# A two-layer vision block on one core: the last pass keeps the first one's token order

## The reference

```
x = x + L0_conv(_ln_c(x))     # 8x8 windows shifted by (4, 4), 12 heads of 8, cosine scores,
                              # a position bias made from a small MLP, a mask across the shift
t = t + L0_ffn(_ln_t(t))      # weights binarized in 5 groups; outputs scaled by the absolute
                              # maximum over 3 images (images 0 to 14 in 5 groups; image 15 gets 0)
x = x + L1_conv(_ln_c(x))     # q = x @ w_q; a 3x3 grouped convolution of q, layer norm, gelu;
                              # offset = tanh(t @ w_offp) * (8, 8); k and v from a bilinear sample
                              # of x at position + offset; 12 heads over all 256 tokens
t = t + L1_ffn(_ln_t(t))      # 4 experts of 384, the best 2 by softmax gate
```

## Time and profile before

| | us |
|---|---|
| three runs | 1008.96, 1015.61, 1023.27 |
| median | 1015.61 |
| profiled execution | 1014.97 |
| its span, first to last instruction | 1013.1 |
| TensorE busy, matmuls | 802.2 (79%) |
| VectorE, ScalarE, GpSimd busy | 490.8, 444.0, 354.3 |
| mean granted TensorE clock | 0.925 of full speed |

### The profile page before, as it was taken

One profiled execution on the slowest core, in us unless ns is written; L12 is line 12 of the kernel. 1 busy time (PEld: TensorE's weight loads), 2 busy tenths in 40 slices (PEclk: granted clock), 3 DMA queues, 4 the chain that ended last, 5 costly groups with the idle time before them and its releaser, 6 DMA issues.

```text
span 1013.1 us, 27125 instructions
## 1 busy us (share of the span) xinstructions
PE 802.2 (79%) x11232; PEld 622.7 (61%) x11232; DVE 490.8 (48%) x1080; ACT 444.0 (44%) x690; POOL 354.3 (35%) x866
## 2 busy tenths in 40 slices
PE   3466776276828875897799898499999999999998
PEld 2345555164616753675777666377777787776766
DVE  3244454263428616674536733455664465465411
ACT  0233352152305431752585483145435444553573
POOL 3335445353424504631512221224423322331233
PEclk9999888597959996998899998799999899999999
DMA  7000000004003033510130400442144044404000
GB/s 218 23 2 4 3 3 7 20 2 103 6 20 85 21 80 90 126 44 19 40 69 6 102 4 25 114 103 68 41 105 106 13 95 106 99 22 91 6 6 12
DMA packets 23450, 53.45 MB, mean 53 GB/s; under 512 B 9552, under 2 KB 18080, under 8 KB 21280
## 3 DMA queue, kind: packets, MB, share of 16 engines
q1 hardware_dynamic: 22752, 51.47, 21.3%
q10 hardware_dynamic: 576, 0.25, 0.1%
HBM read 45.40 MB, written 6.30 MB: 51 GB/s over the span
## 4 chain that ended last, share of the span: by engine, by line
PE 38%; DMA 7%; issue 4%; DVE 4%; SPq 3%; POOL 3%; ACT 2%; POOLq 0%; ACTq 0%; DVEq 0%
PE ps L1214 35%; DMA hx<-hat_scratch 5%; SPq L473 3%; PE ps L1221 1%; DVE nmx L936 1%; DMA hat_scratch<-hat 1%; ACT prob L1169 1%; DVE hat L917 0%; DVE hat L916 0%; DMA x_all<-x_scratch 0%; ACT L1169 0%; PE ps L1476 0%; PE ps L1270 0%; PE ps L1506 0%; ACT L1196 0%
## 5 line engine op out<-in xcount | busy, mean ns | idle before, releaser
L936 DVE TENSOR_REDUCE nmx<-ps 128x4 f32<-128x1024 f32 x96 | 114.4, 1220 | 50.2 <-PE ps L1214 49.8
L1196 ACT ACTIVATE hidden<-ps 128x512 f32<-128x512 f32 x96 | 57.2, 597 | 142.2 <-PE ps L1214 141.9
L1214 PE MATMUL ps<-turned_x,we 128*128 128x256 f32 x384 | 104.6, 397 | 0.0
L1214 PE MATMUL ps<-we,hidden 128*128 128x96 f32 x768 | 103.4, 287 | 0.7 <-ACT hidden L1196 0.7
L1214 PEld LDWEIGHTS ps<-we,hidden 128*128 128x128 f32 x768 | 96.9, 200 | 11.0 <-issue 7.1
L1169 ACT ACTIVATE prob<-ps 128x1024 f32<-128x1024 f32 x96 | 93.5, 1025 | 16.3 <-PE ps L1214 15.4
L545 POOL TENSOR_SCALAR veps_c<-mv_c 128x2 f32<-128x2 f32 x32 | 9.3, 290 | 235.5 <-DVE mv_c L711 235.2
L1214 PEld LDWEIGHTS ps<-turned_x,we 128*128 128x128 f32 x384 | 67.4, 194 | 17.0 <-issue 7.6
L1214 PE MATMUL ps<-wconv,xpp 128*128 128x96 f32 x576 | 71.6, 286 | 4.2 <-POOL xpp L631 3.7
L1214 PE MATMUL ps<-u_turned 32*64 32x64 f32 x3072 | 52.9, 238 | 27.1 <-DVE nmx L936 17.7
L1214 PEld LDWEIGHTS ps<-wconv,xpp 128*128 128x128 f32 x576 | 69.8, 202 | 7.1 <-POOL xpp L631 4.1
(11 more groups left out here) (230 smaller groups left out, 1616.4 us busy)
## 6 DMA issues: line engine op xcount, KB each, us to landing
hx<-hat_scratch SPq DMA_DIRECT2D x16, 1536.0 KB, 12.7
hy<-hat_scratch SPq DMA_DIRECT2D x16, 768.0 KB, 5.9
hat_scratch<-hat SPq DMA_DIRECT2D x32, 96.0 KB, 1.9
x_scratch<-x_all SPq DMA_DIRECT2D x128, 6.0 KB
x_all<-in_x SPq DMA_DIRECT2D x4, 384.0 KB, 4.3
x_all<-x_scratch SPq DMA_DIRECT2D x16, 96.0 KB, 1.9
out<-u_hid SPq DMA_DIRECT2D x16, 96.0 KB, 1.7
x_scratch<-x_all SPq DMA_DIRECT2D x64, 12.0 KB
```

What stands on the lines that cost most here:

```text
L936: v.tensor_reduce(dst, src, AX.X, ALU.max, negate=True).then_inc(sem("c_mx"), 1)
L1196: a.activation(hidden[:, 2 * k:2 * k + 2, :].rearrange("p m n -> p (m n)"), ps[:, k % 2, :], ACT.Gelu).then_inc(sem("c_h"), 1)
L1214: return m.matmul(o, l, r, start=start, stop=stop)
```

## The change

1. **The host's layout is read and written in window order to the end.** Within a window the 64 tokens are now numbered row by row (`j // 8`, `j % 8`; before, four columns at a time), and the result is put back into raster order by the host. `leave`, `back`, `x2_scratch` and the semaphores for them are gone; `c_st` waits for `b_x2` (or `a_x1` for image 15) instead.
2. **The convolution's raster copy is made on chip.** `c_xt` transposes the two tiles twice, the second time with a reordered output; `c_xnt` copies the first result to a new tile `cxt`, which `c_q` reads; a new ScalarE piece `c_xp` makes `xpp` from the second with four copies, turning rows and columns by the shift.
3. **The coordinates come back in another form.** `hx` now has one tile's size and `hy` two: six transfers of 64 partitions each, in place of two of 128.
4. **Set-up functions are tied to pieces of image 0** (`run`), so that `a_xt(0)`, `a_xnt(0)` and others no longer stand behind them; `table_2` is half as many flip matmuls, twice as wide. The convolution's weights have a semaphore of their own (`inw`) and are folded at image 4, not 2.
5. **All five tables are new.** Two lines of `PLAN_PE`:

The diff, cut to its core:

```diff
@@ tiles
-        hx = sb("hx", [P, TILES * DG * TOK])
-        hy = sb("hy", [P, DG * TOK])
+        hx = sb("hx", [P, DG * TOK])
+        hy = sb("hy", [P, TILES, DG * TOK])
+        cxt = sb("cxt", [P, TOK])
@@ run
-            for n, (_, name, i) in enumerate(turns(plan)):
-                for f in set_up.get(n, ()):
-                    f()
+            for _, name, i in turns(plan):
+                if i == 0:
+                    for f in set_up.get(name, ()):
+                        f()
                 pieces[name](i)
@@ SyncE
-            def leave(i):
-                w("b_x2" if fed(i) else "a_x1", i)
-                image = x2_dram[TOK * i:TOK * i + TOK, :].rearrange("(r c) k -> r c k", c=SIDE)
...
-                            sp.dma_start(image[a0:a0 + rows, c0:c0 + 4, :], x_all[p0:p0 + 4 * rows, i, t, :]).then_inc(landed("x2_out", i), 16)
-
-            def back(i):
-                sp.wait_ge(*at("x2_out", i))
-                w("x_back", i - 1)
-                sp.dma_start(x_all[:, i], x2_dram[TOK * i:TOK * i + TOK, :].rearrange("(p t) k -> p t k", t=TILES)).then_inc(sem("x_back"), 16)
@@ hin
-                yrow = bass.AP(d.tensor, d[0].offset, [[DG * TOK, SIDE], [0, 8], [1, DG * TOK]])
-                xrow = bass.AP(d.tensor, d[1].offset, [[0, SIDE], [2 * DG * TOK, 8], [1, 2 * DG * TOK]])
-                sp.dma_start(hy[:], yrow).then_inc(landed("hat_in", i), 16)
-                sp.dma_start(hx[:], xrow).then_inc(landed("hat_in", i), 16)
+                line = DG * TOK
+                for win in range(2):
+                    part = slice(WIN * win, WIN * win + WIN)
+                    cols = bass.AP(d.tensor, d[1].offset + 8 * win * line, [[0, 8], [line, 8], [1, line]])
+                    sp.dma_start(hx[part, :], cols).then_inc(landed("hat_in", i), 16)
+                    for t in range(TILES):
+                        rows = bass.AP(d.tensor, d[0].offset + 8 * t * line, [[line, 8], [0, 8], [1, line]])
+                        sp.dma_start(hy[part, t, :], rows).then_inc(landed("hat_in", i), 16)
@@ GpSimd
             def c_sh(i):
-                pool.wait_ge(*at("c_xnt", i))
+                pool.wait_ge(*at("c_xp", i))
...
-                     c_ln3=c_ln3, c_rank=c_rank, c_acc=c_acc), PLAN_POOL, {1: [late]})
+                     c_ln3=c_ln3, c_rank=c_rank, c_acc=c_acc), PLAN_POOL, {"a_ln2": [late]})
@@ VectorE
             def c_st(i):
-                dve.wait_ge(*at("x_back", i))
+                w("b_x2" if fed(i) else "a_x1", i)
...
-            run(pieces, PLAN_DVE, {1: [weights_1, weights_2, weights_3, bias_8]})
+            run(pieces, PLAN_DVE, {"a_ss": [weights_1], "a_qn": [weights_2], "a_mx": [weights_3, bias_8]})
@@ ScalarE
             def c_xnt(i):
                 act.wait_ge(*at("c_xt", i))
-                w("c_q", i - 2)
+                w("c_q", i - 1)
+                a.copy(cxt[:], ps[:, 2, 0:TOK]).then_inc(sem("c_xnt"), 1)
+
+            def c_xp(i):
+                act.wait_ge(*at("c_xt", i))
                 w("c_conv", i - 2)
-                a.copy(xpp[:, i % 2, 1:3, 8:8 + P], ps[:, 2, 0:TOK].rearrange("p (a n) -> p a n", a=2)).then_inc(sem("c_xnt"), 1)
+                half, low = SIDE // 2, SHIFT // 2
+                turned_rows = ps[:, 2, TOK:2 * TOK].rearrange("p (r n a) -> p a r n", a=2, n=half)
+                planes = xpp[:, i % 2, 1:3, 8:8 + P].rearrange("p a (r n) -> p a r n", n=half)
+                for r0, r1, rt in ((0, SIDE - SHIFT, SHIFT), (SIDE - SHIFT, SIDE, 0)):
+                    for n0, n1, nt_ in ((0, half - low, low), (half - low, half, 0)):
+                        a.copy(planes[:, :, rt:rt + r1 - r0, nt_:nt_ + n1 - n0], turned_rows[:, :, r0:r1, n0:n1]).then_inc(sem("c_xp"), 1)
...
-            run(pieces, PLAN_ACT, {0: [table_1, table_2, bias_exp, signs]})
+            run(pieces, PLAN_ACT, {"a_xnt": [table_1], "a_qt": [table_2], "a_nmt": [bias_exp], "a_ot": [signs]})
@@ TensorE
-                    for ch in range(2):
-                        src = ebraw[:, 6 * b:6 * b + 6, :].rearrange("p h (r c) -> p h r c", c=15)[:, :, :, 4 * ch:4 * ch + 4]
-                        for h in range(6):
-                            ins = mm(ps[:, 6 + b, WIN * h + 32 * ch:WIN * h + 32 * ch + 32], flip[:], src[:, h])
+                    src = ebraw[:, 6 * b:6 * b + 6, :].rearrange("p h (r c) -> p h r c", c=15)[:, :, :, 0:8]
+                    for h in range(6):
+                        ins = mm(ps[:, 6 + b, cols(h, WIN)], flip[:], src[:, h])
...
-                banks.take([2], "c_xnt", i)
-                turn(2, pads["c_xn"][:, i % 2]).then_inc(sem("c_xt"), 1)
+                banks.take([2], "c_xp", i)
+                src = pads["c_xn"][:, i % 2]
+                turn(2, src)
+                for t in range(TILES):
+                    o = ps[:, 2, TOK + P * t:TOK + P * t + P].rearrange("p (r w n) -> p w r n", r=8, w=2)
+                    ins = m.transpose(o, src[:, t, :], ident[:])
+                ins.then_inc(sem("c_xt"), 1)
...
-                    ins = mm(flat(0, 1024)[:, cols(g, TOK)], wqs[:, g, :], xpp[:, i % 2, 1:3, 8:8 + P])
+                    ins = mm(flat(0, 1024)[:, cols(g, TOK)], wqs[:, g, :], cxt[:])
...
-            run(pieces, PLAN_PE, {0: [table_1, table_2]})
+            run(pieces, PLAN_PE, {"a_xt": [table_1], "a_tk": [sums], "a_tq": [table_2]})
```

More of the change, by code:

```diff
@@ L45 @@
 PLAN_PE = """
[L46 to L50, removed]
@@ L69 @@
[L69 to L74, removed]
@@ L75 @@
[L75 to L79, removed]
@@ L212 @@
 """
 PLAN_SP = """
-leave 123.80 124.85 127.32 195.63 197.32 199.15 265.19 267.02 268.71 335.50 337.25 339.02 480.24 482.54 483.82 486.06
-back 127.16 128.21 130.68 198.99 200.68 202.51 268.55 270.38 272.07 338.86 340.61 342.38 483.60 485.90 487.18 489.42
-hout 164.82 225.76 264.79 276.91 298.12 381.62 438.32 498.46 523.61 557.25 590.86 624.47 658.08 690.63 724.05 757.47
-hin 167.28 228.22 267.82 291.58 312.63 384.08 440.78 500.92 526.07 559.71 593.32 626.93 660.54 693.09 726.51 759.93
-store 378.50 435.18 482.06 517.59 557.45 591.06 624.67 658.28 691.39 724.81 758.23 789.22 818.43 838.32 852.61 866.61
+hout 147.62 169.56 234.15 273.79 301.54 355.35 426.28 499.81 554.00 591.29 630.45 667.36 703.87 740.38 776.89 813.40
@@ L220 @@
+hin 150.88 172.82 237.41 277.05 304.80 358.61 429.54 503.07 557.26 594.55 633.71 670.62 707.13 743.64 780.15 816.66
+store 372.35 434.18 507.01 554.90 580.46 636.51 673.96 709.93 746.44 782.95 819.46 838.55 867.81 886.95 901.41 914.66
 """
@@ L362, in build_program @@
         made = {}
-        counts = dict(a_mx=2, a_exp=2, c_xn=2, c_cn=2, c_mx=6, c_exp=6, c_pv=3, c_h=6, c_w=3, c_y=2, c_ym=2, c_s=3, c_st=3, a_pb=2, c_up=6,
-                      a_mv=2, a_mv2=2, c_mv=2, c_cmv=2, c_mv3=2, c_sh=2, x2_out=192, x_back=16, hat_out=32, hat_in=32, done=16, wc_set=2)
-        moved = ("x2_out", "hat_out", "hat_in", "done")
+        counts = dict(a_mx=2, a_exp=2, c_xn=2, c_cn=2, c_mx=6, c_exp=6, c_pv=3, c_h=6, c_w=3, c_y=2, c_ym=2, c_s=3, c_st=3, a_pb=2, c_xp=4, c_up=6,
+                      a_mv=2, a_mv2=2, c_mv=2, c_cmv=2, c_mv3=2, c_sh=2, hat_out=32, hat_in=96, done=16, wc_set=2)
+        moved = ("hat_out", "hat_in", "done")
         RING = 2
@@ L498, in store @@
                 sp.dma_start(out[TOK * i:TOK * i + TOK, :].rearrange("(p t) k -> p t k", t=TILES), acc[:, i % 2]).then_inc(landed("done", i), 16)
-            run(dict(leave=leave, back=back, hout=hout, hin=hin, store=store), PLAN_SP, {})
+            run(dict(hout=hout, hin=hin, store=store), PLAN_SP, {})
             for i in range(IMAGES - RING, IMAGES):
@@ L510, in _ @@
             own.mark(g.memset(neghalf[:], -0.5))
+            own.mark(g.memset(w2s[:].rearrange("p m n -> p (m n)"), 0.0))
             own.mark(g.memset(nst[:].rearrange("p t n -> p (t n)"), 0.0))
@@ L1616, in _constants, with _places @@
     return c
+def _places():
+    import numpy as np
+    tile, part = np.arange(TILES), np.arange(P)
+    win, j = part // WIN, part % WIN
+    r, col = j // 8, j % 8
+    R = (SHIFT + 8 * tile[None, :] + r[:, None]) % SIDE
+    K = np.broadcast_to(((SHIFT + 8 * win + col) % SIDE)[:, None], R.shape)
+    return R, K
 def _layout(a):
@@ L1720 @@
     r = _run(nc, [arrays], core_ids=[0])
-    return _np.asarray(r.results[0]["out_0"]).reshape(IMAGES, SIDE, SIDE, C)
+    R, K = _places()
+    laid = _np.asarray(r.results[0]["out_0"]).reshape(IMAGES, P, TILES, C)
+    image = _np.empty((IMAGES, SIDE, SIDE, C), laid.dtype)
+    image[:, R, K, :] = laid
+    return image
```

343 lines of the change are left out of this document (174 added, 169 removed).

## The result

The changed kernel takes 1036.96 us, the median of 4 runs (1034.85 to 1041.77), against 1015.12 us of before (1008.96 to 1023.27, 4 runs): a ratio of 1.022, with a 95% interval of 1.014 to 1.030. It is slower; whether by more than 2%, the interval leaves open. The forecast was 1060. The profiled execution is one of 1041.77 us with a span of 1040.0.

A forecast was written before the change was run, and what follows sets the result against it. TensorE's work was taken to bound the late part, waits the early part. From 1015 us, trip, set-up and transposes gave 921; the coordinates' return added 101 and 38, making 1060 us, range 940 to 1100.

The forecast's parts named there:

- the price of the coordinates' return: TensorE waits for coordinates returned on eight DMA engines: +101 us in images 9 to 15, +38 in images 1 to 8.
- the chain that has to be hidden: From `c_offs` through the coordinates' return and three products: 25.6 us at its shortest, plus 10.6 for eight engines, 36.2.
- The base without it: Whole kernel without the price of the coordinates' return: 1015 - 75.5 - 10 - 18 + 10 = 921 us.
- Images 9 to 15, +101: Late images wait 83 us for coordinates, and 2.5 us go to the slow clock after each wait: +101 us.
- Images 1 to 8, half of 75: Early images wait 75 us for coordinates; TensorE idles there anyway, so half was taken: +38 us, bounds 0 and 75.
- The trip: Removing the transfers through DRAM ends five TensorE gaps, -75.5 us, and the slow clock after four of them, -10.
- Set-up: At the start, bias work tied to pieces lets the first scores come at 31 us: -18 us, bounds -13 and -19.
- Transposes: Two more transposes per image on TensorE for the on-chip raster copy, 32 x 0.31: +10 us.
- In the old order 35.0 us of work stand between `c_offs` and `c_sm` in the steady part: hidden: TensorE pieces queued there were said to cover the coordinates' return before; the new order has 24.3 us of cover.
- B (shorter packets): Coordinates' return on half the engines with shorter packets, data in 15 to 16 us: 990 us, chance 0.14.
- C (the eight keep the rate): Coordinates' return on eight engines as fast as on sixteen, waits 10 to 20 us in all: 935 us, chance 0.20.
- D (the gaps come back): Group ends still stop TensorE through the scale chain; half of the 75.5 us return: 1098 us, chance 0.08.

The follow-up runs named there:

- the one with sixteen: Changed kernel with window tokens numbered column by column, coordinates returned in three transfers over 128 partitions with outermost extent 16: 914.54 us, ratio 0.898 against before.
- the first experiment: Changed kernel with column-by-column window tokens, so the coordinates return with outermost extent 16 instead of 8: 914.54 us.
- the last version: Column-by-column kernel without the second pair of transposes, pixels sorted by six strided copies, return cut into six half-line transfers over 128 partitions: 895.56 us, ratio 0.881.

## Why the prediction was right or wrong

Direction and cause were right, the size was not: 4.4% slower was forecast, 2.2% measured. **The step that failed is the price of the coordinates' return**, +139 in the sum and +122.4 measured (1036.96 - 914.54); inside it, the chain that has to be hidden was taken as 36.2 us and is 32.6. The base without it was 6.5 us too high on top. A loss of 122 stands against a gain of about 100 here, so that an error of 23 us in sum halves what is left.

**The coordinates.** Windows from the start to the `c_offs` of image 9, and from there to the end, in the changed kernel and then in the one with sixteen:

```profile
0.00:664.21 664.21, 511.47 (x8580) 395.45 (x8580) 329.92 (x762) 305.91 (x515) 243.82 (x632) 0.89 0.19 46
664.21:1040.00 375.79, 309.15 (x2665) 236.87 (x2661) 153.09 (x318) 162.87 (x254) 83.78 (x234) 0.92 0.22 52
...
0.00:609.59 609.59, 496.78 (x8579) 389.18 (x8579) 331.81 (x762) 305.95 (x515) 251.76 (x632) 0.93 0.21 51
609.59:912.00 302.41, 295.84 (x2665) 231.57 (x2661) 153.65 (x318) 162.50 (x254) 102.15 (x234) 1.00 0.27 64
```

Two terms went wrong, in opposite directions (the two profiled executions differ by 128.0 us, their medians by 122.4).
- *Images 9 to 15, +101, measured +73* (375.8 - 302.4), or 10.5 us an image for my 14.4. The waits ahead of `c_sm`, 83 us in the sum, are 60.1 (7.5 to 9.5 an image); the clock behind them, 17.5, is 13.3, the growth of TensorE's busy time. The engines' part was right: first issue to product 12.5 and 22.8 us, 10.3 more for my 10.6, share 0.52 for 0.54. The term that was too large is the chain itself, "25.6 us at its shortest". I took it from the old pair of transfers, where `hx` lands 17.3 us after `hout`; in the new form, at full engines, the last lands at 802.00 - 787.21 = 14.8 us. Another 0.7 us are the way from `c_offs` to `hout`, 3.9 us for my 4.6. So the chain from `c_offs` to `c_sm` is 32.6 us (798.72 to 831.28), not 36.2; over a cover of 24.3 that makes 8.3 us of waiting.
- *Images 1 to 8, half of 75, measured +55* (664.2 - 609.6). TensorE's idle time grows by 39.9 us there, nearly the 38 of the sum. That this half was right owes something to luck: the 75 came from the chain that was too long. What was missing is the clock, a term that I put at nothing in this part: TensorE's busy time grows by 14.7 us, at a mean clock of 0.89 for 0.93. Between 195 and 652 us there are seven gaps of 6.6 to 10.0 us, where the kernel with sixteen has three of 6.0 to 6.5.

**The base, 921 us, was nearly right**: the kernel with everything but the eight engines takes 914.5. *The trip*, -85.5: -85.0, and right in its parts: without it TensorE idles 76.8 us less and is busy 7.9 us less. *Set-up*, -18: -15.1 alone. *Transposes*, +10: +10.4, in part by luck. I multiplied 32 by the length of one, but two overlap, and the earlier trace rows has 7.1 us for the 32; the second pair is busy for 6.6 us, and without it TensorE's busy time falls by 6.1 (792.6 to 786.5). The rest is idle time that no run explains. These three make 928 from the 1017.7 us of before beside those runs, and 914.5 is 13 us better. TensorE's idle time comes out as the parts have it (210.9 us before, less 76.8, less 14.8 for the set-up: 119.3, measured 119.4), so it is busy time that is shorter. 5.1 us of it are the scores' 34.89 against 29.78, the flips that the new order halves; of the rest no run tells where it comes from. The forecast put nothing on the five new tables, and no run has them alone.

**"In the old order 35.0 us of work stand between `c_offs` and `c_sm` in the steady part: hidden" gave the wrong reason**, though no number of the sum hung on it. The short transfer is hidden there, but with eight engines the old order loses more than the new, 149 us for 122. Pieces ahead of `c_sm` on TensorE are no cover when one of them needs VectorE, and VectorE stands at the product. I had written that "all behind `c_w0` waits too" and did not count it. In the new order the two ways of counting nearly agree, as `c_sm` follows the product closely there (10.44 us of VectorE's waiting, 8.76 of TensorE's).

**Rivals.** B (shorter packets) and C (the eight keep the rate) fall with the share of 0.52, the 22.8 us and the equal packet times: half the engines moved half as much, 119 GB/s for 243. By the Trainium skill ("DMA: Bandwidth & Descriptors", section "Why a DMA increments its semaphore by 16 and not by 1") the largest number up to 16 that divides both slowest dims works: 8 here and 16 in the column order, which is what the two shares show. The rate for 64 partitions in the Trainium skill's page "SBUF — State Buffer" (Door 1, the DMA port swizzle), 196 GB/s, was not reached: 119. D (the gaps come back) falls with the first experiment: no gap over 6.5 us is left in the part of the groups once the transfer is short.

## What to carry to other kernels

When a new data order changes the outermost extents of a transfer, look at the share of the DMA engines that it keeps busy, and pick the order that keeps all 16: here one swap of row and column inside a window turned +2% into -10%, with an otherwise equal change. And the cover of a transfer is counted on the engine that consumes it, from issue to consumer in that engine's own order; if other engines need what is queued behind the consumer, move the consumer back.

## What the runs showed of the hardware that was not expected

A mixture of one transfer in three on eight engines and the rest on sixteen was slower than a sum of the packets gives: share 0.71 to 0.84 and 17.9 us, for 15.9 worked out, with a fifth more time for the same packets. A transpose that writes its 128 columns in rows of eight takes the same 273 ns as a plain one, and so does one that writes each column 16 elements from the last, in the kernel with sixteen outermost. Two gaps of nearly the same length cost differently: behind 8.1 us of idle TensorE the clock was 0.50 for 10 us in the old order, behind 8.8 us it was 0.70 over 5 us in the new. Six strided copies of 16 to 96 elements per partition took 0.71 us of ScalarE together (a line of the last version):

```profile
701.49 0.71 ACT L1131 COPY xpp<-ps 128x96 f32<-128x96 f32 x6
```
